# Grouped-query layer of a four-layer kernel: values of two key tiles weighed one behind the other, four buffers of probabilities in place of two

## What is computed

```python
q = rope(x @ Wq); k = rope(x @ Wk); v = x @ Wv      # 16, 4 and 4 heads
out = softmax(q @ k.T / 4) @ v                       # no mask, 512 keys
return out.reshape(...) @ Wo
```

## Time and profile before

| | us |
|---|---|
| median of 3 runs | 3229.29 (3227.49 to 3232.86) |
| span of the profiled execution | 3162.5 |
| around the span (median less span) | 66.8 |
| PE busy in the span | 2888.1 (91%) |
| DVE busy | 1857.3 (59%) |
| ACT busy | 1374.4 (43%) |

### The profile page before, as it was taken

How to read it: one execution, slowest core, us unless ns; L and a number is a source line. 1 busy time by engine, 2 the same in 40 slices (tenths; PEclk the granted TensorE clock), 3 DMA queues, 4 the chain that set the end, 5 groups by cost and what they waited for, 6 DMA issues and landing times.

```text
span 3162.5 us, 50664 instructions
## 1 busy us (share of the span) xinstructions
PE 2888.1 (91%) x14374; PEld 1806.1 (57%) x14407; DVE 1857.3 (59%) x4478; ACT 1374.4 (43%) x1985; POOL 328.3 (10%) x353
## 2 busy tenths in 40 slices
PE   5999999999988888888879999999999499999998
PEld 2455545545544444443447777766666366666666
DVE  5656565665637777777747777762222555555552
ACT  1534453454333555555545554532233144444443
POOL 0000000000000000000021211121111311111110
PEclk7999999999986999999999999999999699999999
DMA  6434542553402112221214111132212443434440
GB/s 213 128 101 108 153 127 70 151 154 99 114 29 85 56 57 68 68 67 56 68 50 162 46 53 42 38 110 74 93 63 67 104 96 89 94 88 95 95 95 15
DMA packets 144298, 279.77 MB, mean 88 GB/s; under 512 B 22384, under 2 KB 80112, under 8 KB 134160
## 3 DMA queue, kind: packets, MB, share of 16 engines
q1 hardware_dynamic: 131760, 244.90, 26.9%
q0 software_dynamic: 10464, 28.59, 3.2%
q10 hardware_dynamic: 2016, 5.58, 0.5%
HBM read 179.31 MB, written 99.68 MB: 88 GB/s over the span
## 4 chain that ended last, share of the span: by engine, by line
PE 71%; DVE 13%; issue 5%; DMA 5%; ACT 3%; POOL 2%; SPq 1%; DVEq 0%; ACTq 0%; POOLq 0%
PE bank_u L559 7%; PE pair L599 5%; PE pair L543 5%; PE pair L700 4%; PE pair L1984 4%; PE bank L488 3%; DVE nmax L870 3%; PE pair L2911 3%; PE bank_m L2875 3%; PE bank L2426 3%; PE pair L744 3%; PE bank L2875 3%; PE bank L520 2%; PE pair L499 2%; PE pair L1406 2%
## 5 line engine op out<-in xcount | busy, mean ns | idle before, releaser
L776 ACT ACTIVATE probs<-pair 128x1024 f32<-128x1024 f32 x512 | 501.0, 1020 | 216.1 <-PE pair L543 215.1
L870 DVE TENSOR_REDUCE nmax<-bank 128x1 f32<-128x512 f32 x664 | 441.8, 685 | 211.6 <-PE bank L520 149.4
L870 DVE TENSOR_REDUCE nmax<-bank_m 128x1 f32<-128x512 f32 x360 | 246.5, 685 | 112.9 <-PE bank_m L520 66.9
L559 PE MATMUL bank_u<-probs,vext 128*32 128x512 f32 x2048 | 293.8, 648 | 0.6 <-ACT uraw L763 0.5
L520 PE MATMUL bank<-k_a,q_a 96*128 96x512 f32 x336 | 173.4, 551 | 23.3 <-DMA k_a<-parts_dram 19.9
L543 PE MATMUL pair<-q_a,k_a 98*128 98x512 f32 x512 | 173.9, 447 | 17.1 <-ACT probs L776 11.8
L2116 DVE CUSTOM_DVE_ANT_0 bank<-bank,mask_q 128x128 f32<-128x128 f32 (+1 forms) x320 | 118.4, 416 | 78.4 <-PE bank L1888 77.5
L543 PEld LDWEIGHTS pair<-q_a,k_a 98*128 98x128 f32 x512 | 90.2, 201 | 114.2 <-ACT probs L776 65.6
L2019 ACT ACTIVATE probs<-pair 128x896 f32<-128x896 f32 x128 | 115.1, 919 | 73.5 <-PE pair L1906 73.5
L1379 PE MATMUL bank<-k,q 62*128 62x512 f32 x302 | 114.5, 483 | 26.7 <-DVE nmax L870 26.7
L1984 PE MATMUL pair<-fc,hid 128*128 128x256 f32 x512 | 131.2, 382 | 6.0 <-ACT probs L2019 6.0
(11 more groups left out here) (432 smaller groups left out, 5845.0 us busy)
## 6 DMA issues: line engine op xcount, KB each, us to landing
parts_dram<-parts SPq DMA_DIRECT2D x64, 512.0 KB, 2.9
q_a<-parts_dram SPq DMA_DIRECT2D x31, 512.0 KB, 5.2
k_a<-parts_dram SPq DMA_DIRECT2D x31, 512.0 KB, 7.1
q<-parts_dram SPq DMA_DIRECT2D x97, 128.0 KB, 2.6
xs<-xres SPq DMA_DIRECT2D x24, 512.0 KB, 3.0
xl<-xs SPq DMA_DIRECT2D x24, 512.0 KB, 3.9
x_in<-xg SPq DMA_DIRECT2D x74, 128.0 KB, 2.1
yg_dram<-y_out POOLq DMA_DIRECT2D x72, 128.0 KB, 2.0
```

Of the source, the lines that this page charges most:

```text
L559: ins = nc.tensor.matmul(bank_u[32 * h:32 * h + 32, :], vext[:, kt, kv(g, h), :], probs[:, kt % 2, h * SEQ:(h + 1) * SEQ], start=(kt == 0) ...
L776: nc.scalar.activation(probs[:, kt % 2, hp * 2 * SEQ:hp * 2 * SEQ + n], st.tile(l, name)[:, 0:n], ACT.Exp).then_inc(st.free["act"].sem, 1)
L870: nc.vector.tensor_reduce(nmax[:, g % 2, qt, h:h + 1], sc.tile(l, name)[:], AX, ALU.max, negate=True).then_inc(sc.free["dve"].sem, 1)
```

## The change

In PRE1 and MAIN1 (`deep`) a second tensor `probs_b` holds key tiles 2 and 3, in the space of a tensor that was unused, so four key tiles of probabilities can be live. Steps with odd kt weigh nothing; steps with even kt weigh the two tiles of the two steps before, one behind the other; the last two are weighed behind group 3. `act_exp` waits for the weighing of four tiles before instead of two. POST1 keeps the old order, and PRE1 has no back half, so the 7 rounds of MAIN1 are what changes.

```diff
+        def deep(l):
+            return l in (PRE1, MAIN1)
+        def probs_at(l, kt):
+            return probs_b[:, kt - 2, :] if deep(l) and kt > 1 else probs[:, kt % 2, :]
...
-                                       probs[:, kt % 2, h * SEQ:(h + 1) * SEQ], start=(kt == 0), stop=(kt == TT - 1))
+                                       probs_at(l, kt)[:, h * SEQ:(h + 1) * SEQ], start=(kt == 0), stop=(kt == TT - 1))
...
-                act.wait_ge(*pv_done.at(l, it, max(0, TT * g + kt - 1)))
-            nc.scalar.activation(probs[:, kt % 2, hp * 2 * SEQ:hp * 2 * SEQ + n], st.tile(l, name)[:, 0:n],
+                act.wait_ge(*pv_done.at(l, it, max(0, TT * g + kt - (3 if deep(l) else 1))))
+            nc.scalar.activation(probs_at(l, kt)[:, hp * 2 * SEQ:hp * 2 * SEQ + n], st.tile(l, name)[:, 0:n],
...
-        spare_q = sb("spare_q", [P, 8 * SEQ], F32, l1)
+        probs_b = sb("probs_b", [P, 2, GH * SEQ], F32, l1)
...
-                    if back and (g or kt):
-                        pe_weigh(pe, l, it, GROUPS * g + kt - 1, kv_of_group)
+                    if back and (g or kt) and not (deep(l) and kt % 2):
+                        for n in (2, 1) if deep(l) else (1,):
+                            pe_weigh(pe, l, it, GROUPS * g + kt - n, kv_of_group)
...
-                pe_weigh(pe, l, it, GROUPS * TT - 1, kv_of_group)
+                for n in (2, 1) if deep(l) else (1,):
+                    pe_weigh(pe, l, it, GROUPS * TT - n, kv_of_group)
```

## The result

The changed kernel takes 3261.49 us (median of 4 runs, 3258.55 to 3263.15) against 3228.39 us before (3220.03 to 3232.86): a ratio of 1.0106, with an interval of 1.0090 to 1.0123. It is 33 us slower, where 18 were forecast.

What follows compares the result with a forecast made beforehand. Hops with a weighing were taken as bound by TensorE's work, those without by a TensorE-VectorE loop. Place-by-place terms gave +2.5 us a round, +17.8 over 7 rounds on 3229.3: 3247.1 us, range 3226 to 3266.

Steps and rivals of the forecast that it cites:

- The price of the second weighing: A weighing directly behind another in MAIN1 costs 0.87 us, with bounds 0.65 and 1.00; one alone takes 1.00.
- The floor of a hop: Between maxima score pairs, a hop without a weighing takes 1.29 us, set by scores, VectorE's reduction and hand-over.
- The round, place by place: Gains and losses at each place of a MAIN1 round, summing to +2.5 us a round, +17.8 for 7 rounds.
- group 0, transposes to projection: Group 0: fewer weighings, but the projection needs its score pair back from ScalarE; -0.2 us, bounds 0 and -1.0.
- logits to GRU's matmuls: Group 1, kt 2 and 3: +0.87 for a second weighing, 1.00 saved ahead of the GRU's matmuls; -0.13 us.
- behind group 3: A second weighing ahead of scores that started with no idle time; +0.87 us a round.
- The loosened wait is worth nothing: ScalarE's exponentials wait for scores; no wait for a weighing is among the leading ones, so loosening it gains nothing.
- the clock falls more often: Rival, chance 0.20: added TensorE waits bring half-clock stretches to five more rounds, 2.9 us each, 14.5 on top: 3262.
- What lies around the span: 66.8 us of the measured time were taken to lie around the profiled span of 3162.5 us.
- TensorE's busy time: Sign in a changed MAIN1 round: TensorE's busy time down by some 2 us, idle time up by more than 4.
- TensorE's work decides: Rival, chance 0.09: 8 borders saved per round give 0.32 us each, 17.9 us in all, 3211.4.
- the loss is taken up: Rival, chance 0.09: later waits inside a round swallow the loss, gains and losses cancel: 3229, within 3223 to 3236.

Runs made afterwards that it cites:

- e5: Kernel before with 16 useless score matmuls during TensorE's wait for the normalised input in each MAIN1 round: 3159.82 us against 3164.93, ratio 0.9984.
- the last experiment: Kernel before with doubled weighings at two places a round plus 16 useless matmuls during the wait for the normalised input: 3202.63 us against 3217.52, ratio 0.9948.

## Why the prediction was right, and where it fell short

The direction, the mechanism of the waits and the range were right; the number was 14 us low, because a loss by the clock stood in a side case and not in the sum. By its own steps:

- **The price of the second weighing.** Taken 0.87 from layer 3, measured 0.86 (1.86 for two). Right.
- **The floor of a hop.** Taken 1.29, measured 1.29. Right; the shortened reductions move it as said. Three such hops in a row were expected; there are two, and the third is longer by other work in it.
- **The round, place by place**, from the timelines at equal clock but for the first (us, start to start):

| place | forecast | measured |
|---|---|---|
| group 0, transposes to projection | -0.2 | +0.2 (8.23 to 8.40) |
| projection to logits | 0 | 0.0 (18.01 to 17.99) |
| logits to GRU's matmuls | -0.13 | -0.4 (5.51 to 5.12) |
| group 2, kt 0 and 1 | +0.5 | +0.5 (7.08 to 7.61) |
| group 2, kt 2 and 3 | +0.5 | +0.7 (5.03 to 5.69) |
| group 3 | +1.0 | +0.9 (13.29 to 14.23) |
| behind group 3 | +0.87 | +0.86 (2.00 to 2.86) |
| sum | +2.5 | +2.8; the round at clock 0.96: +2.7 |

The first place is read in two rounds with equally long slow stretches there. Where the stretch is shorter, in the last of the six rounds, it takes 7.08 (1541.17 to 1548.25), and group 2 has the rest of the slow time; so the 2.7 of that round confirms the total, not the places. In every round the projection now stands some 0.65 us for ScalarE's exponentials.

- **The loosened wait is worth nothing.** Right, 1.0000 for the buffers alone.
- **The clock.** This step failed. The sum of the prediction put the clock at nothing: it held the clock fixed in its likeliest case and set "the clock falls more often" apart as a rival of 0.20, with 3262. That rival is what happened, 3261.5. Its size was near (14.5 forecast, 12 measured), its form was not: not five more rounds with one 2.9 us stretch at the logits, but a second fall in every round, of varying length and in two places. The mistake was the weighting. The trace before had shown, in one of six rounds, a fall behind TensorE's standing twice at the logits; the change adds such waits in groups 1 to 3 in every round. The two cases exclude each other only if waits and clock are independent, and the repeated scores show that they are not: with the waits filled by work there are fewer falls and a shorter time, in two orders.
- **What lies around the span.** 66.8 us was wrong (1.7). It did no harm, since the sum was added to the median.
- **TensorE's busy time.** This sign did not come. It was to fall by some 2 us a round and the idle time to rise by more than 4; in rounds of equal clock TensorE is busy for 73.40 in place of 73.53 and idle for 2.8 more. The runs don't show where the time saved at the borders went.
- **Rivals.** That TensorE's work decides fell: 8 borders are saved and the kernel is slower. The Trainium skill, TensorEngine Tiling (Array Packing), section Tiling Modes, says that a change of tiling mode drains the engine. The trace agrees that a border costs (a weighing takes 1.00 alone, 0.86 directly behind another); whether a drain is the reason no run here shows. What was saved was worth less than the wait that the weighing had been filling. That the loss is taken up fell too: five of the seven places are longer.

## What to carry to other kernels

Before packing like work together, look at what it stood between: work in the slack of a loop between two engines is free where it is, and moved it costs its whole length there, while the hops that it left only fall to the loop's floor. Put a pair where a wait of another kind or a stretch of pure TensorE work takes it, and leave the rest. Count the waits that a change makes as more than their length, when the profile shows the clock falling behind such waits: add the half-clock price of what follows as part of the forecast, not as a side case, and try matmuls of no use in the waits, since here they won time in three kernels.

## What the runs showed of the hardware

**Useless matmuls made a kernel faster.** Twenty a round won 18 us in one order (ratio 1.0106 to 1.0048), sixteen in an otherwise unaltered kernel 5 us. But taking one fall away can bring another later in the round, as in e5.

**Layer 3 differs from chip to chip.** The kernel before took 3228, 3165 and 3218 us in the three sets, each on one chip. The profile of the buffers alone, whose span is 3223.2, has a wait in layer 3 that the profile before, at 3162.5, has not (waits of ACT: total, times, longest):

```profile
ACT probs L2029 <- remote: 45.4, 7, 7.7
```

"remote" says that the profile names no engine of this core as the releaser. The wait stands in the rounds of layer 3 between ScalarE's activation table load and its first exponential, while GpSimd issues eight indirect DMAs. Rounds of layer 3 are 81.2 us apart without it and about 89 with it. No profile of the set at 3165 us has it; those of the set at 3218 do (36.9 us, 7 times, in the last experiment). What ScalarE waits for there, and why on some chips only, was not tried.
